# Softmax normalisation of an attention layer moved from VectorE to GpSimd

## The reference, cut to what matters

```python
q = _rms_norm(q, g_q)
k = _rms_norm(k, g_k)
logits = jnp.einsum('bhqd,bhkd->bhqk', q, k) * d ** (-0.5)
attn = jax.nn.softmax(logits, axis=-1)
o = jnp.einsum('bhqk,bhkd->bhqd', attn, v)
...
return o + o @ W_out
```

## Time and profile before

| | |
|---|---|
| median of three runs | 3099.62 us |
| the profiled execution, its own time | 3095.6 us |
| span of its trace | 3093.5 us |
| mean granted TensorE clock | 0.93 |

### The profile page before, as it was taken

One profiled execution on the slowest core, in us unless ns is written; L12 is line 12 of the kernel. 1 busy time (PEld: TensorE's weight loads), 2 busy tenths in 40 slices (PEclk: granted clock), 3 DMA queues, 4 the chain that ended last, 5 costly groups with the idle time before them and its releaser, 6 DMA issues.

```text
span 3093.5 us, 130035 instructions
## 1 busy us (share of the span) xinstructions
PE 2879.0 (93%) x47184; PEld 2502.9 (81%) x47184; DVE 1746.1 (56%) x6459; ACT 1065.8 (34%) x4862; POOL 1284.5 (42%) x3409
## 2 busy tenths in 40 slices
PE   6899999999999556899999999999999999999998
PEld 4368777767778455899999899899899899899987
DVE  1636644644642444566666666666666666666654
ACT  1122332543442122333333333333333333333322
POOL 0000000100110466666666566566566566656600
PEclk7589999999999655799999999999999999999999
DMA  4613312532532000244444444444344444444466
GB/s 146 201 38 103 99 58 67 183 95 88 184 101 75 25 0 0 71 128 130 135 129 126 127 131 128 125 130 127 119 139 127 123 130 128 119 135 129 129 215 203
DMA packets 137146, 359.18 MB, mean 116 GB/s; under 512 B 16016, under 2 KB 24848, under 8 KB 136592
## 3 DMA queue, kind: packets, MB, share of 16 engines
q1 hardware_dynamic: 136336, 353.72, 37.7%
q10 hardware_dynamic: 672, 3.67, 0.3%
HBM read 322.85 MB, written 34.47 MB: 116 GB/s over the span
## 4 chain that ended last, share of the span: by engine, by line
PE 60%; DVE 3%; issue 2%; ACT 1%; DMA 0%; DVEq 0%; POOL 0%; ACTq 0%; SPq 0%; POOLq 0%
PE pscan L1019 13%; PE pscan L1015 13%; PE pg L946 11%; PE pd L972 11%; PE pu L946 11%; ACT th L869 1%; DVE state L1176 1%; DVE qraw L1176 0%; PE prouter L1029 0%; PE prouter L1037 0%; DMA wgu<-w_split 0%; PE pd L1044 0%; DVE pscan L1162 0%; DVEq L1175 0%; DVE th L1159 0%
## 5 line engine op out<-in xcount | busy, mean ns | idle before, releaser
L1015 PEld LDWEIGHTS pscan<-th,clo 128*128 128x128 f16 x16384 | 555.8, 97 | 143.5 <-ACT th L869 123.0
L1015 PE MATMUL pscan<-th,clo 128*128 128x8 f16 x16384 | 564.3, 167 | 109.8 <-ACT th L869 109.8
L1019 PE MATMUL pscan<-th,chi 128*128 128x16 f16 x16384 | 561.5, 170 | 3.0 <-DVE th L1159 2.3
L1019 PEld LDWEIGHTS pscan<-th,chi 128*128 128x128 f16 x16384 | 486.8, 97 | 4.5 <-DVE th L1159 4.5
L946 PE MATMUL pg<-qh,wgu 128*128 128x256 f16 x3168 | 430.5, 275 | 16.7 <-issue 15.8
L972 PE MATMUL pd<-hg,wd 128*128 128x256 f16 x3168 | 429.8, 275 | 2.2 <-DMA wd<-w_split 2.2
L946 PE MATMUL pu<-qh,wgu 128*128 128x256 f16 x3168 | 426.3, 274 | 0.0
L869 ACT ACTIVATE th<-state 128x32 f16<-128x32 f32 x768 | 175.9, 229 | 719.3 <-DVE state L1176 719.1
L1176 DVE TENSOR_REDUCE state<-pscan 128x32 f32<-128x96 f32 x768 | 197.4, 257 | 265.0 <-PE pscan L1019 259.7
L946 PEld LDWEIGHTS pg<-qh,wgu 128*128 128x128 f16 x3168 | 295.5, 98 | 55.9 <-issue 17.2
L946 PEld LDWEIGHTS pu<-qh,wgu 128*128 128x128 f16 x3168 | 294.1, 98 | 34.0
(11 more groups left out here) (164 smaller groups left out, 4286.8 us busy)
## 6 DMA issues: line engine op xcount, KB each, us to landing
wgu<-w_split SPq DMA_DIRECT2D x264, 512.0 KB, 3.6
wd<-w_split SPq DMA_DIRECT2D x264, 384.0 KB, 3.1
part_in<-in_w_tiles SPq DMA_DIRECT2D x120, 256.0 KB, 3.0
w_split<-part_out SPq DMA_DIRECT2D x99, 256.0 KB, 2.8
late<-in_w_tiles SPq DMA_DIRECT2D x78, 256.0 KB, 3.0
w_split<-late SPq DMA_DIRECT2D x33, 128.0 KB, 3.3
hid<-in_up_q SPq DMA_DIRECT2D x8, 512.0 KB, 4.0
hid<-in_up_s SPq DMA_DIRECT2D x16, 256.0 KB, 5.5
```

The lines of the kernel that those rows point to most:

```text
L1015: mm(pscan[:, 0, m * B:(m + 1) * B], clo[:, k, m * P:(m + 1) * P], th[:, k, 0, :], start=(m == 0 and k == 0), stop=False, skip_group_check ...
L1019: ins = mm(pscan[:, 0:2, m * B:(m + 1) * B], chi[:, k, m * P:(m + 1) * P], th[:, k], start=False, stop=(k == NC - 1), skip_group_check=True)
```

## The change

The two multiplications of each head, 256 instructions in all, leave VectorE's `normed` and become `divided` on GpSimd, which waits for the reciprocals (`d_rinv`) and signals `d_pn`. VectorE keeps maxima, reciprocals, copies and the expert parts. GpSimd's own work is put in line with that: the scale stands behind the 64 heads of batches 0 to 3, and in batches 4 to 7 the `third` of a piece split at head h stands just ahead of `divided` of head h + 2.

```diff
--- before.py
+++ after.py
@@ -218,6 +218,21 @@
             pl.affine_select(out=hv, in_=hv, compare_op=ALU.is_ge, fill=0.0, base=DH - 1,
                              pattern=[[DH, HPC], [0, DH]], channel_multiplier=-1).then_inc(S["eye"], 1)
 
+            def divided(b, h):
+                pl.wait_ge(S["d_rinv"], b * HEADS + h + 1)
+                for qc in range(2):
+                    ins = pl.tensor_scalar(pr[:, h % HPC, qc, :], pr[:, h % HPC, qc, :], rinv[:, h, qc:qc + 1], None, ALU.mult)
+                ins.then_inc(S["d_pn"], 1)
+
+            def third_part(tile):
+                pl.wait_ge(S["part_hi"], 3 * tile + 3)
+                if tile:
+                    pl.wait_ge(S["third_out"], 16 * tile)
+                pl.tensor_scalar(third, part_out[2][:, 0, :], 2.0 ** -11, None, ALU.mult).then_inc(S["part_third"], 1)
+
+            for b in range(4):
+                for h in range(HEADS):
+                    divided(b, h)
             pl.wait_ge(S["widest"], 1)
             steps = [0]
             def link(ins):
@@ -234,11 +249,15 @@
             link(pl.tensor_scalar(ki[:, 0:1], ki[:, 2:3], -2.0 ** 23, float((254 + 13) << 23), ALU.mult, ALU.add))
             link(pl.tensor_scalar(ki[:, 1:2], ki[:, 2:3], 2.0 ** 23, float((13 + Q_BITS) << 23), ALU.mult, ALU.subtract))
             pl.sem_inc(S["wscale"], 1)
-            for tile in range(TILES):
-                pl.wait_ge(S["part_hi"], 3 * tile + 3)
-                if tile:
-                    pl.wait_ge(S["third_out"], 16 * tile)
-                pl.tensor_scalar(third, part_out[2][:, 0, :], 2.0 ** -11, None, ALU.mult).then_inc(S["part_third"], 1)
+            for b in range(4, B):
+                for h in range(HEADS):
+                    for n in split_parts(b, h - 2) if h > 1 else split_parts(b, -1) if h == 1 else []:
+                        if n % 3 == 2:
+                            third_part(n // 3)
+                    divided(b, h)
+                for n in split_parts(b, HEADS - 2) + split_parts(b, HEADS - 1):
+                    if n % 3 == 2:
+                        third_part(n // 3)
 
         @block.scalar
         def _(act):
@@ -560,10 +579,6 @@
                 def normed(h):
                     dve.wait_ge(S["a_exp"], b * HEADS + h + 1)
                     dve.reciprocal(rinv[:, h, :], psum_e[:, h, :]).then_inc(S["d_rinv"], 1)
-                    dve.wait_ge(S["d_rinv"], b * HEADS + h + 1)
-                    for qc in range(2):
-                        ins = dve.tensor_scalar(pr[:, h % HPC, qc, :], pr[:, h % HPC, qc, :], rinv[:, h, qc:qc + 1], None, ALU.mult)
-                    ins.then_inc(S["d_pn"], 1)
                 def turned(h):
                     if not ffn and h + NC < PIECES:
                         restore(h + NC)
```

## The result

The changed kernel takes 3131.59 us (median of 4 runs, 3128.82 to 3134.70), the kernel before 3099.35 us beside it: ratio 1.0105, 95% interval 1.0093 to 1.0116. It is slower by 32 us where I forecast 12.2. The sign was right and the time lies inside the range, but the size is missed by more than half. The likeliest case of the prediction was not what happened; the time is the one that its rival of the 16-bit pace named (3125 to 3142 us).

The account below looks back on a forecast made before the run. TensorE, busy 93%, bounds the kernel, so only its waits for multiplied heads count. Terms 3.4 + 0 + 0.5 + 4.5 + 2.8 + 1 = 12.2 us on 3099.6 give 3112 us, range 3094 to 3136.

Parts of the forecast that it names:

- likeliest case of the prediction: Whole kernel: GpSimd multiplies at 476 ns an instruction, time 3112 us, own range 3106 to 3120; chance 0.40.
- rival of the 16-bit pace: GpSimd multiplies at the pace of a 16-bit row: sum 25 to 42 us, time 3125 to 3142 us; chance 0.20.
- One instruction is 476 ns: One 256-element multiplication on GpSimd: 400 ns of work plus 76 for the scalar; the pair 0.95 us.
- My charge for the scalar: GpSimd multiplication: reading one scalar from a tile adds 76 ns, at most 152.
- The upper end, 962 ns: One GpSimd multiplication priced from a 16-bit row: 962 ns, the pair 1.92 us; the forecast took the lower 476.
- point 1: Batches 1 to 3, position 2: late by 0.50 - 0.22 = 0.28 us in 12 quads, +3.4 us (+1.6 to +15).
- Positions 1 and 3: Batches 1 to 3: position 1's longer multiplication is hidden; position 3's reciprocal starts 0.53 us sooner, covering the 0.50: 0.
- Batch 0: Only its last quad waits for multiplications: about one latency, +0.5 us, up to +3.
- The scale: It moves behind head 63 on GpSimd; another 7 us is hidden by over 30 us: 0.
- Points 4 and 5: Batches 4 to 7: existing multiplication waits grow, +4.5 us; queueing behind third parts adds +2.8 in batch 6, +1 elsewhere.
- Contention: VectorE and GpSimd hold each other up at 2 instructions per quad in 16 quads: +12 us, 3124; chance 0.07.

## Why the prediction missed

**Length of a multiplication: the step that failed.** "One instruction is 476 ns" was built on a slope between the earlier trace rows. The earlier trace rows is a select and the earlier trace rows a clamp with minimum and maximum: two operations, neither of them a multiplication. The clamp took 214 ns at 32 elements, the multiplication takes 287. The one row of the same operation was the earlier trace rows, and I put it aside because it has 16 bits; f16 and f32 take the same 848 ns at 256. The price was 476 ns where 922 came, the pair 0.95 us where 1.84 came, and every term that holds a latency was too small. My charge for the scalar was right (76, measured 72 to 74). The upper end, 962 ns, was within 5% of the 922 measured. The Trainium skill's rule (GPSIMD Engine Reference, 4.1 Engine selection), one input at about line rate, is not what the runs show: 922 ns against 352 on VectorE, and over 512 elements the product of two inputs is shorter (1038) than the multiplication by one constant (1487).

**Position 2 in batches 1 to 3.** The mechanism and the place were right. With the measured latency the sum of point 1 is (1.28 - 0.22) x 12 = 12.7 us, and 12.0 came out, of 3.4 forecast. That the two are so close is in part luck. By the run with positions 0 and 1 alone, 1.7 of the 12.0 us belong to position 0 of the first quads, which I had put at nothing (the earlier trace rows show the fourth quad); position 2 then lost 10.3 us, 0.86 a quad. So it had some 0.4 us to spare and not 0.22, as the run with one product says too (0.47 us later, 0.07 lost). Positions 1 and 3 were 0, as forecast.

**Batch 0 and the scale.** Nothing can be read in batch 0 above its spread. The scale cost nothing that shows: with GpSimd multiplying in batches 0 to 3 only, batches 4 to 7 were 1.7 us longer.

**Batches 4 to 7.** Points 4 and 5 had 8.3 us, 24 at the upper ends; 27.7 came. One place was right: in batch 6 a third part stands ahead of position 3 in all four quads and ends where the pair starts (807.07 and 807.06 us in the first). The other third part of each of those quads, ahead of position 1, I had left out for batch 6, and for batches 4 and 7 had counted as some tenths unless the pair took 1.92 us; at 1.84 us it made TensorE wait 5.9 us in the three. What was too small is what GpSimd's queue holds in a quad. I had asked of each head how late it gets; the pairs of 1.84 us and the thirds of 1.48 us stand in one line, and a stretch of it as in batch 4 above leaves no gap to catch up. The thirds' length is the larger part of this, shown by cutting it: 27.7 became 10.0 us. One difference I had not priced works the other way: TensorE's waits for the ReLU went from 10.6 to 0.9 us. With the shorter product the four batches lost 9.1 us, near the 8.3 of my sum, which was made for such a length; the whole run lost 5 to 6 us of the 12.2, so for its own length the sum was about twice too high.

**Contention.** Given 0.07 as a rival, it is real beside the length. A GpSimd multiplication that meets the end of one low part and the whole of the next took 1623 ns instead of 922, the difference 701 being close to the whole of a low part (744), and one that meets a low part already begun is late by what is left of it, less 0.13 us. That is the rule of the Trainium skill (SBUF — State Buffer, "SBUF: two separate sides"), by which whichever of the two starts first holds a shared port for the whole instruction, and the trace agrees. The same section names a second case, a VectorE instruction in a mode that takes both ports; the 162 ns beside VectorE's one-input multiplication follow the same 0.13 us and would fit it, but no run here shows in which mode VectorE worked. The worth of the contention, up to 8 us, overlaps with that of the thirds, since both lengthen one queue; the shares of latency, thirds and contention in the 27.7 us do not add up and were not parted further. Of the 17 us that positions 0 and 1 alone cost in these batches, TensorE's waits name 10.6, the largest rise being at position 1 behind a third part (from 0 to 7.8 us); the rest is open.

## What to carry to other kernels

Price an instruction from a row of the same operation on the same engine, even where type and size differ, before one that only looks alike in type; where the two ends lie a factor of 2 apart and the sum hangs on it, the upper end deserves its chance. Work moved to an idle engine is late by its whole latency, hand-off included, at every place where the consumer had no slack, so idle time of the new engine is no argument. And before it joins a queue that holds another engine's buffer, add up what the queue has to do between two due times: here a third part ahead of the multiplication delayed TensorE, and behind it ScalarE, at 42 us more.

## What the runs showed of the hardware

- GpSimd, one input of 128 partitions by one scalar: 209 ns and 2.50 ns an element, 74 ns more with the scalar from memory, the same for 16 and 32 bits (848 ns at 256).
- GpSimd's product of two inputs was shorter: 723 ns at 256 elements, 1038 at 512 with one input broadcast; a copy of 512 took 609. One broadcast product replaced two multiplications of 922 ns and won back 27 us of the 32.
- GpSimd and VectorE in SBUF at once: a multiplication of 922 ns became 1450 when it began 0.08 us after a two-input instruction of 744, 1623 beside two of these in a row, and 1084 when it began 0.06 us after a one-input one of 353. In the first and the last case it is late by what VectorE had left at its start, less 0.13 us. Beside a one-input reduction of VectorE of 675 ns no multiplication took more than 947 ns.
- GpSimd started 0.09 us after the recorded end of VectorE's reciprocals (258.89 + 0.16 to 259.14, and 0.09 to 0.10 us in all 72 heads in which it stood idle), less than the 0.21 us of the earlier trace rows.
